# Decay logarithms from running sums by one product over 128 rows, and a running state that is kept turned

## The chip, the cores and the metric

The kernel is one program on one core of a Trainium2 chip. The metric is device time in microseconds (us) of one execution. Three runs of the kernel before gave 4488.98, 4490.3 and 4494.2 us, median 4490.3 us.

## The reference

The program computes one layer of a hybrid model in four steps, each `x = x + f(layernorm(x))`: a state-space mixer, a feed-forward part, a long convolution with a gate, and the same feed-forward part again. `x` is 8 sequences of 2048 tokens of 256 numbers. The change touches the mixer. For every sequence and every one of 8 heads it keeps a state `h` of 64 x 128 numbers:

```
B_proj, C_proj = turned by cos/sin of cumsum(dt * theta)   # 8 heads x 128
alpha = exp(dt_t * A_neg)
beta  = (1.0 - lam_t) * dt_t * alpha
gamma = lam_t * dt_t
h   = alpha * h + beta * Bx_prev + gamma * Bx_t            # Bx_t = u_t (64) times B_t (128)
y_t = einsum('bhpn,bhn->bhp', h, C_t)
```

`y` then goes through an RMS norm and an output projection. The kernel takes 128 tokens (a tile) at a time. Within a tile, token t gets from token s the product C_t.B_s times `exp(sum of the log alphas of s+1..t)`, and from all earlier tiles `exp(sum of log alphas up to t)` times C_t times the state at the tile's start. The sums of log alphas between two tokens are what the code calls decay logarithms; the state at the tile's start is the running state.

## The kernel before, in words

The program runs in five parts, one after the other: `normalise_tokens` (to about 124 us), `scan_and_filter` (to about 238 us), `mixer_and_first_ffn` (to about 3290 us), `long_convolution`, and `project_and_second_ffn`. In each part every engine has its own list of instructions, written out in order; the engines wait for one another on counting semaphores.

`scan_and_filter` makes all per-token numbers of the mixer for all 128 tiles at once: sigmoids, angles, sums of log alphas over tokens (TensorE products with the triangular matrices `upto` and `after`), exponentials of these. They are laid out in `params_all` (80 columns for each tile, `P_COS` to `P_ET`) and stored to DRAM. Two of the groups of eight columns (`P_A`) are the log alphas themselves, cut into two parts that add up to them.

`mixer_and_first_ffn` goes through the tiles in rounds of four (a quad). The list of one round is `body(tile, quad, n)`: for q = 0 to 3 it calls steps for tile 4n+q (lag 0), the tile before it (lag 1) and two before it (lag 2), and in between steps for whole quads (the first feed-forward part for quad n-1, the wide projection with its short filter for quad n-2). The calls stand in a fixed order for each engine. A step waits with `wait_for(engine, step, i)` until another step is done for tile i. Eight banks of PSUM are shared out: `bank_read` makes a writer wait until the former contents are read. The banks named here are `p_bc` (two), `p_tr` (transposes), `p_arg` (decay logarithms and the new state's product), `p_gram`, `p_y`, `p_post` (two, for the quad steps).

For a tile i the steps that the change touches, or that stand next to them, are these; g = 0, 1 is a group of four heads.
- POOL `masked_steps` (line 1050) multiplies `upto` by the log alphas of each head, twice (two parts): 128 x 512 numbers a time. PE `decay_logs` (lines 729 and 730) multiplies `after_r` by both and adds them up in `p_arg`. ACT `exponentials` (line 908) takes exp, ACT `own_bounds` (line 915) and DVE `cut_decay` (line 1173) bound the result, DVE `weigh_gram` multiplies it with the products C.B (`gram`, line 754).
- PE `turn_over` (line 744) transposes B and C by head through `p_tr`, ACT `copy_turned` (line 924) copies the bank to SBUF. There are four of these for a tile, over one bank.
- PE `outputs` (lines 769 and 772) makes y for four heads: the part from the tile and the part from `state`. It writes two heads beside each other, one into partitions 0 to 63 and one into 64 to 127.
- PE `new_state` (line 780) makes B times u for all eight heads, with B as the stationary operand of 128 x 128 and u as the moving one of 64 columns. POOL `fade_state` (line 1071) has multiplied the old state by its decay, DVE `carry_state` (line 1194) adds the product. `state` has n on the partitions and 8 x 64 columns.
- PE `project_u` (line 736) multiplies x with the weights of u. It stands right behind the last `turn_over` of the tile; behind it come `decay_logs` of group 1, and at q = 0 `x2n_over` (line 833), the transposes of the second layer norm's output, which ACT `normalised` (line 940) makes.

SP issues the loads; the DMAs of one round are the parts of x, `el` (exponentials by row), `par` (a quad's columns of `params_dram`) and the stores.

Of the kernel before, what the change touches and what calls it, by code (L numbers as in the profile page):

```python
# [6 lines left out]
F32 = mybir.dt.float32  # L7
F32R = mybir.dt.float32r
# [16 lines left out]
P_COS, P_SIN, P_A, P_G, P_RHO, P_W, P_EL, P_ET, P_ALL = 0, 8, 24, 40, 48, 56, 64, 72, 80  # L25
P_EARLY = P_G
# [207 lines left out]
def scan_and_filter(nc, ctx, t):  # L234
# [9 lines left out]
    a_hi = sb("sp_a_hi", [128, COLS], F32R)  # L244
# [26 lines left out]
    with nc.Block() as block:  # L271
        @block.sync
        def _(sp):
# [23 lines left out]
            sp.wait_ge(s["stored"], 64)  # L297

        @block.gpsimd
        def _(pool):  # L300
# [5 lines left out]
            g_.tensor_copy(t["after_r"][:, :], t["after"][:, :])  # L306
# [18 lines left out]
            g_.memset(taps[:, :, 0:TOK - 1], 0.0)  # L325
            pool.drain().then_inc(s["weights_done"], 1)

        @block.vector
        def _(dve):
# [44 lines left out]
            v_.tensor_copy(a_hi[:, :], arr["a"][:, :])  # L374
# [37 lines left out]
            v_.tensor_copy(col(P_A), as3(a_hi[:, :].bitcast(F32)))  # L412
            v_.tensor_tensor(col(P_A + HEADS), as3(arr["a"][:, :]), as3(a_hi[:, :].bitcast(F32)), ALU.subtract)
# [11 lines left out]
            dve.wait_ge(s["scan_act"], EXPS)  # L425
            by_seq = params[:, :, :].rearrange("p (b c) n -> p b c n", b=BATCH)
# [12 lines left out]
        def _(act):  # L439
# [32 lines left out]
        def _(pe):  # L472
# [38 lines left out]
            for b in range(BATCH):  # L511
                last = mm(pp[0][:, b * TOK:(b + 1) * TOK], arr["a"][:, b * 128:(b + 1) * 128], t["upto"][:, :], start=True, stop=True)
# [12 lines left out]
def mixer_and_first_ffn(nc, ctx, t):  # L525
# [4 lines left out]
    H64 = GROUP * HEAD_U  # L530
    QUAD = 4
    QUADS = TILES // QUAD
    SPAN = QUAD * TOK
    ident, upto, after, bound = t["ident"], t["upto"], t["after"], t["bound"]

    w_u, w_bc, in_w, after_r = t["w_u_sb"], t["w_bc_sb"], t["in_w_sb"], t["after_r"]
# [11 lines left out]
    steps = two("steps", [128, W4], F32R)  # L548
    decay, own, mix = two("decay", [128, W4]), two("own", [128, W4]), two("mix", [128, W4])
    u_g, u_w, state = sb("u_g", [128, 512]), sb("u_w", [128, 512]), two("state", [128, 512])  # L550
# [16 lines left out]
    names = ("project_b project_c rotate_b rotate_c turn_b turn_c over_b over_c copy_b copy_c steps logs exp diagonal own gram mix outputs take_y "  # L567
             "values gate_values weigh_values new_state fade carry_state split_hi split_rest sum_over mean_sq square_y pair_sums scan_rstd project_out "
             "residual1 rstd1 norm1 xn_over first_column shifted mixed key relu key_sq receptance tanh value gated residual2 rstd2 norm2 "
             "x2n_over x2_hi x2_lo widen took taps halo short_filter setup load_xnT0 load_xnT1 load_par0 load_par1 load_x0 load_x1 load_el0 load_el1 "  # L570
             "store_x2 store_x0 store_vx").split()
    BY_GROUP = set(names[:19])
# [19 lines left out]
    BANK_TR = (("over_c1", "copy_c1", 1, -1), ("over_b1", "copy_b1", 1, -1), ("over_c0", "copy_c0", 1, 0), ("over_b0", "copy_b0", 1, 0))  # L592
# [49 lines left out]
    with nc.Block() as block:  # L642
        @block.sync
        def _(sp):
# [30 lines left out]

            def load_x(n, pp):
# [16 lines left out]
            for i in range(2):  # L693
                load_xnT(i, Place(0, i, 0))
            load_par(0, 0)

            def body(tile, quad, n):
                for q in range(QUAD):
                    tile(q, -2, load_xnT)
                    tile(q, 0, load_el)  # L700
                    if q == 1:
                        quad(-1, load_par)
                        quad(2, store_x2)
                        quad(0, load_x)
# [1153 lines left out]
```

## Time and profile before

| what | value |
|---|---|
| median of three runs | 4490.3 us |
| profiled execution | 4485.84 us |
| its span (first to last instruction) | 4484.1 us |
| mean granted TensorE clock, of full speed | 0.978 |
| PE busy | 4197.9 us, 94% of the span |
| DVE busy | 3222.6 us, 72% |
| POOL busy | 2376.0 us, 53% |
| ACT busy | 2157.4 us, 48% |

Busy time is the time in which an engine runs at least one instruction. PE's matmuls overlap and their ends are modelled, so the cost of one in a dense sequence is read from the distance between two starts. PEld is TensorE's loading of the stationary operand, which overlaps the matmuls. The idle time of an engine says only something about the program's time where this engine's next instruction is on the path that sets the end.

### The profile page before, as it was taken

Reading aid. Unit: us, or ns where it says so; the run is one execution under the profiler, and the core shown is the slowest. Engines: PE = TensorE matmul, PEld = TensorE weight load, DVE = VectorE, ACT = ScalarE, POOL = GpSimd, SP = SyncE. Lnnn points to the kernel's source line nnn. Section 1 sums busy time; section 2 is a strip of 40 time slices with the busy share of each in tenths; the row PEclk is TensorE's granted clock in tenths of the full one; section 3 lists DMA queues with packets and bytes.
Section 4 is the critical chain, followed back from the end, with each engine's and each line's share of the span. In section 5 each row is a group of like instructions: output and inputs, shape, how many; then the busy total and the mean of one; then the engine's idle time right before and its main releaser. Section 6 shows DMA issues by size and latency. Waiting matters only on the chain. (4 is left out here: it accounts for less than half of the span.)

```text
span 4484.1 us, 118726 instructions
## 1 busy us (share of the span) xinstructions
PE 4197.9 (94%) x39924; PEld 3488.0 (78%) x39924; DVE 3222.6 (72%) x6737; ACT 2157.4 (48%) x5046; POOL 2376.0 (53%) x3284
## 2 busy tenths in 40 slices
PE   5389999999999999999999999999869999989999
PEld 3178788888888888878788788888648888878888
DVE  8867777777677776777767777677636666668888
ACT  3234444454444444444444444444446666645555
POOL 3276666666676666766666666666400000026666
PEclk9699999999999999999999999999979999989999
DMA  8321111111111111111111111111056666633333
GB/s 276 117 81 30 48 39 39 47 39 48 36 38 50 39 48 36 39 50 39 39 45 39 50 39 36 48 39 46 23 134 180 188 180 183 186 94 105 105 105 96
DMA packets 369774, 347.50 MB, mean 77 GB/s; under 512 B 24953, under 2 KB 343289, under 8 KB 360185
## 3 DMA queue, kind: packets, MB, share of 16 engines
q1 hardware_dynamic: 352380, 323.98, 24.2%
q10 hardware_dynamic: 16896, 16.78, 1.1%
q8 instruction: 324, 5.31, 0.5%
q14 instruction: 174, 1.43, 0.1%
HBM read 232.01 MB, written 108.66 MB: 76 GB/s over the span
## 5 line engine op out<-in xcount | busy, mean ns | idle before, releaser
L721 PE MATMUL bank<-w_bc,xnT 128*128 128x512 f32 x3072 | 804.3, 404 | 11.7 <-POOL xnT L1042 11.7
L924 ACT COPY turned_t<-bank 128x512 f32<-128x512 f32 x512 | 300.3, 587 | 982.4 <-PE bank L744 982.3
L721 PEld LDWEIGHTS bank<-w_bc,xnT 128*128 128x128 f32 x3072 | 556.8, 189 | 144.7 <-issue 34.5
L1455 PE MATMUL p_yc<-sig,toep 64*64 64x256 f32 (+14 forms) x16384 | 538.1, 282 | 13.7 <-issue 10.5
L1455 PEld LDWEIGHTS p_yc<-sig,toep 64*64 64x64 f32 x16384 | 475.1, 132 | 89.7 <-issue 43.5
L1050 POOL TENSOR_TENSOR steps<-upto,par 128x512 fp32r<-128x512 f32 x512 | 536.6, 1068 | 0.0
L1159 DVE TENSOR_TENSOR rot<-bank,par 128x512 f32<-128x512 f32 x512 | 350.1, 684 | 209.6 <-PE bank L721 124.7
L1059 POOL TENSOR_TENSOR turned_b<-rot 128x512 f32<-128x512 f32 x256 | 325.9, 1273 | 197.7 <-DVE rot L1160 197.5
L1604 POOL MEMSET xT<- 128x258 f32 x1 | 0.3, 314 | 684.2 <-POOLq L1349 684.2
L1059 POOL TENSOR_TENSOR turned_c<-rot 128x512 f32<-128x512 f32 x256 | 354.5, 1385 | 1.8 <-DVE rot L1160 1.8
L1160 DVE TENSOR_TENSOR rot<-bank,par 128x512 f32<-128x512 f32 x512 | 346.9, 677 | 0.0
L1248 DVE SCALAR_TENSOR_TENSOR conv<-bank,short,conv 128x511 f32<-128x511 f32 (+1 forms) x384 | 286.4, 746 | 69.7 <-ACT conv L980 55.4
L840 PE MATMUL bank<-x2T,in_w 128*128 128x512 f32 x1152 | 315.4, 410 | 18.7 <-issue 9.0
L915 ACT ACTIVATE own<-bound,par 128x128 f32<-128x128 f32 x1024 | 326.5, 400 | 0.4 <-DMA par<-params_dram 0.4
L1042 POOL TENSOR_TENSOR xnT<-xnT_raw,xnT 128x256 fp32r<-128x256 f32 x128 | 108.8, 850 | 384.2 <-ACT xnT L903 384.2
L1179 DVE TENSOR_TENSOR mix<-bank,decay 128x512 f32<-128x512 f32 x256 | 175.3, 685 | 180.1 <-PE bank L754 175.5
L754 PEld LDWEIGHTS bank<-turned_t 128*128 128x128 f32 x2048 | 265.3, 191 | 31.8 <-ACT turned_t L924 13.0
L754 PE MATMUL bank<-turned_t 128*128 128x128 f32 x2048 | 273.5, 276 | 0.7 <-DVE u_g L1167 0.4
L840 PEld LDWEIGHTS bank<-x2T,in_w 128*128 128x128 f32 x1152 | 214.9, 191 | 69.6 <-issue 21.4
L1487 DVE TENSOR_TENSOR ys<-p_yc,odd_y 64x256 f32<-64x256 f32 x256 | 95.6, 411 | 235.8 <-ACT odd_y L1406 235.8
L780 PEld LDWEIGHTS bank<-u_w,turned_b 128*128 128x128 f32 x2048 | 248.5, 192 | 10.3 <-issue 0.2
L1091 POOL TENSOR_TENSOR rstd<-var_eps,minus_half 128x2 f32<-128x2 f32 x128 | 90.7, 708 | 294.8 <-DVE var_eps L1205 291.7
(264 smaller groups left out, 9671.5 us busy)
## 6 DMA issues: line engine op xcount, KB each, us to landing
toep<-taps_dram SPq DMA_DIRECT2D x256, 260.0 KB, 4.1
el<-el_dram SPq DMA_DIRECT2D x256, 128.0 KB, 3.0
xg<-arg_x SPq DMA_DIRECT2D x32, 512.0 KB, 5.1
xnT_dram<-xt_g ACTq DMA_DIRECT2D x32, 512.0 KB, 5.4
xnT_raw<-xnT_dram SPq DMA_DIRECT2D x128, 128.0 KB, 2.5
x_quad<-arg_x SPq DMA_DIRECT2D x32, 512.0 KB, 3.9
x_dram<-x_quad SPq DMA_DIRECT2D x32, 512.0 KB, 3.7
x0T_dram<-conv SPq DMA_DIRECT2D x32, 512.0 KB, 2.8
```

What stands on the lines that cost most here:

```text
L721: last = mm(p_bc[c][:, :], xnT[w.q % 2][p][:, k, :], w_bc[q][:, k, c * 1024 + g * W4:c * 1024 + (g + 1) * W4], start=(n == 0), stop=(n == ...
L754: last = mm(p_gram[:, c], turned_t[g][0][:, c], turned_t[g][1][:, c], start=True, stop=True)
L780: last = mm(p_state[:, v], turned(w, h // GROUP, 0)[:, (h % GROUP) * STATE:(h % GROUP + 1) * STATE], u_w[:, v], start=True, stop=True)
L840: last = mm(p_post[W_BANK[e]][:, :], in_w[q][:, k, e * 128:(e + 1) * 128], x2T[p][:, k, :], start=(m == 0), stop=(m == len(SPLIT) - 1))
L915: last = s_.activation(own[g][:, h * TOK:(h + 1) * TOK], bound[:, :], ACT.Identity, scale=par[w.p][:, w.q, P_RHO + g * GROUP + h:P_RHO + g ...
L924: s_.copy(turned_t[g][c][:, :], p_tr[:, :]).then_inc(s[f"copy_{BC[c]}"], 1)
L1050: last = g_.tensor_tensor(heads(steps[p][:, :]), upto[:, :].unsqueeze(1).broadcast_to([128, GROUP, TOK]), over(of_group(P_A + p * HEADS, w ...
L1059: g_.tensor_tensor(turned(w, g, c)[:, :], rot1[c][:, :], rot2[c][:, :], ALU.add).then_inc(s[f"turn_{BC[c]}"], 1)
L1159: v_.tensor_tensor(heads(rot1[c][:, :]), heads(p_bc[c][:, :]), cos, ALU.mult)
L1160: v_.tensor_tensor(parts(rot2[c][:, :]), parts(p_bc[c][:, :])[:, :, ::-1, :], over(sin.rearrange("p (h s) -> p h s", s=2), STATE // 2), AL ...
L1248: last = v_.scalar_tensor_tensor(out=conv[:, e, back:], in0=p_post[W_BANK[e]][:, 0:SPAN - back], scalar=short[:, e, 2 - back:3 - back], in ...
L1455: last = mm(by_seq(p_y[p][c][odd * H:(odd + 1) * H, 0:2 * TILES])[:, :, first:], toep[n % SLOTS][c * H:(c + 1) * H, lag * H:(lag + 1) * H] ...
```

## The change: what it does, and the diff

The decay logarithm between s and t is now the difference of two running sums, cum[t] - cum[s]. `scan_and_filter` makes the running sums for all tiles (row = tile and head, column = token), splits them into four pieces so that each is held well in the reduced format `F32R`, and stores them in `cum_dram`. In the mixer one product over 128 rows gives the logarithms of four heads: of its rows, 48 are 4 pieces times (8 rows for heads: cum[s] on one side, minus one for the head on the other; 4 rows for the tiles of the quad: cum[t] on one side, a one for the tile on the other), 16 are zero, and 64 put -1e30 where t < s for pairs of tokens. The fixed rows come from a new input `pick` by two loads at the part's start and are copied by ACT into `sums_s` and both buffers of `sums_t`; SP loads the other rows for each quad by eight DMAs (`load_sums`). `masked_steps`, `P_A` and `after_r` are gone.

The running state is now accumulated as `state_p`, with u on the partitions (two heads above each other) and n in the columns. `new_state` has u as the stationary operand of 64 columns and B as the moving one of 128. `outputs` still needs the other layout, so PE turns the state for each tile (`turn_state`, four transposes through `p_tr`) and ACT copies it (`copy_state`).

```diff
-P_COS, P_SIN, P_A, P_G, P_RHO, P_W, P_EL, P_ET, P_ALL = 0, 8, 24, 40, 48, 56, 64, 72, 80
+P_COS, P_SIN, P_G, P_RHO, P_W, P_EL, P_ET, P_ALL = 0, 8, 24, 32, 40, 48, 56, 60
+PIECES, GRID = 4, 98304.0
 # scan_and_filter, SP
+            for p in range(PIECES):
+                sp.dma_start(t["cum_dram"][p].rearrange("(b c) n -> c b n", c=128), cum[p][:, :].rearrange("c (b n) -> c b n", b=BATCH)).then_inc(s["stored"], 16)
 # scan_and_filter, POOL, at its end
+            pool.wait_ge(s["scan_dve"], LOGS)
+            g_.tensor_scalar(coarse[:, :], arr["a"][:, :], GRID, None, ALU.add)
+            g_.tensor_scalar(coarse[:, :], coarse[:, :], GRID, None, ALU.subtract)
+            g_.tensor_tensor(fine[:, :], arr["a"][:, :], coarse[:, :], ALU.subtract)
 # scan_and_filter, DVE
-            v_.tensor_copy(a_hi[:, :], arr["a"][:, :])
-            v_.tensor_copy(col(P_A), as3(a_hi[:, :].bitcast(F32)))
-            v_.tensor_tensor(col(P_A + HEADS), as3(arr["a"][:, :]), as3(a_hi[:, :].bitcast(F32)), ALU.subtract)
             dve.wait_ge(s["scan_act"], EXPS)
+            for k in range(2):
+                v_.tensor_tensor(cum[2 * k + 1][:, :].bitcast(F32R), pp[1 + k][:, :], cum[2 * k][:, :], ALU.subtract)
 # scan_and_filter, ACT
-            s_.activation(col(P_EL), as3(pp[0][:, :]), ACT.Exp).then_inc(s["scan_act"], 1)
+            s_.activation(col(P_EL), as3(pp[0][:, :]), ACT.Exp)
             s_.activation(col(P_W), as3(pp[1][:, :]), ACT.Exp)
-            s_.activation(col(P_ET), as3(pp[2][:, :]), ACT.Exp)
+            for e in range(2):
+                rows = slice(e * HEAD_U, (e + 1) * HEAD_U)
+                s_.activation(params[rows, :, P_ET:P_ET + HEADS // 2], as3(pp[2][rows, :])[:, :, e::2], ACT.Exp)
+            act.drain().then_inc(s["scan_act"], 1)
             act.wait_ge(s["scan_pe"], ROWS)
             s_.activation(el_rows, pp[0][:, :].rearrange("p (b n) -> p b n", b=BATCH), ACT.Exp)
+            for k in range(2):
+                s_.copy(cum[2 * k][:, :].bitcast(F32R), pp[1 + k][:, :])
 # scan_and_filter, PE
-            for b in range(BATCH):
-                last = mm(pp[0][:, b * TOK:(b + 1) * TOK], arr["a"][:, b * 128:(b + 1) * 128], t["upto"][:, :], start=True, stop=True)
+            for dst, src in ((pp[0], arr["a"]), (pp[1], coarse), (pp[2], fine)):
+                for b in range(BATCH):
+                    last = mm(dst[:, b * TOK:(b + 1) * TOK], src[:, b * 128:(b + 1) * 128], t["upto"][:, :], start=True, stop=True)
 # mixer, SP; load_sums(0, 0) behind load_par(0, 0), then quad(-1, load_sums) behind quad(-1, load_par) at q == 1
+            def load_sums(n, pp):
+                wait(sp, s["picked"], 1)
+                wait_for(sp, "logs1", QUAD * (n - 1) - 1)
+                for p in range(PIECES):
+                    tiles = t["cum_dram"][p, n * SPAN // TOK * HEADS:(n + 1) * SPAN // TOK * HEADS, :]
+                    at = p * (HEADS + QUAD)
+                    sp.dma_start(sums_t[pp][at + HEADS:at + HEADS + QUAD, :, :].bitcast(F32), ...)
+                    sp.dma_start(sums_s[at:at + HEADS, pp * QUAD:(pp + 1) * QUAD, :].bitcast(F32), ...)
+            sp.dma_start(gate[:, :, :], t["pick"][0:128]...).then_inc(s["load_pick"], 16)
+            sp.dma_start(k_sq[:, :, :], t["pick"][128:256]...).then_inc(s["load_pick"], 16)
             load_par(0, 0)
+            load_sums(0, 0)
 # mixer, PE
             def decay_logs(i, w, g):
-                wait_for(pe, f"steps{g}", i)
+                wait(pe, s["picked"], 1)
+                wait(pe, s[f"load_sums{w.p}"], 16 * 2 * PIECES * (w.n // 2 + 1))
                 bank_read(pe, BANK_ARG, f"logs{g}", i)
-                mm(p_arg[:, :], after_r[:, :], steps[0][:, :], start=True, stop=False)
-                mm(p_arg[:, :], after_r[:, :], steps[1][:, :], start=False, stop=True).then_inc(s["logs"], 1)
+                mm(p_arg[:, :], sums_s[:, w.p * QUAD + w.q, :], sums_t[w.p][:, g, :], start=True, stop=True).then_inc(s["logs"], 1)
             def outputs(i, w, g):
-                wait_for(pe, "carry_state", i - 1)
+                wait_for(pe, "copy_state", i - 1)
             def new_state(i, w):
                 for h in range(HEADS):
-                    last = mm(p_state[:, v], turned(w, h // GROUP, 0)[:, ...], u_w[:, v], start=True, stop=True)
+                    pair, e = h // 2, h % 2
+                    last = mm(p_state[e * 64:(e + 1) * 64, pair * STATE:(pair + 1) * STATE], u_w[:, h * HEAD_U:(h + 1) * HEAD_U],
+                              turned(w, h // GROUP, 0)[:, ...], start=True, stop=True)
+            def turn_state(i, w):
+                wait_for(pe, "carry_state", i)
+                bank_read(pe, BANK_TR, "turn_state", i + 1)
+                for pair in range(4):
+                    c = slice(pair * 128, (pair + 1) * 128)
+                    last = tp(p_tr[:, c], state_p[1 - w.q % 2][:, c], ident[:, :])
+                last.then_inc(s["turn_state"], 1)
                     tile(q, 0, project_u)
+                    tile(q, 1, turn_state)
 # mixer, ACT
+            def copy_state(i, w):
+                wait_for(act, "turn_state", i)
+                wait_for(act, "outputs1", i - 1)
+                s_.copy(state[1 - w.q % 2][:, :], p_tr[:, :]).then_inc(s["copy_state"], 1)
+            act.wait_ge(s["load_pick"], 32)
+            s_.copy(sums_s[:, :, :], flat_k.rearrange("r (m n) -> r m n", n=TOK))
+            for p in range(2):
+                s_.copy(sums_t[p][:, :, :], flat_gate.rearrange("r (g n) -> r g n", g=GROUPS))
+            act.drain().then_inc(s["picked"], 1)
                     tile(q, 0, copy_turned, 0, 0)
+                    tile(q, 1, copy_state)
 # mixer, POOL (masked_steps and its two calls are gone)
             def fade_state(i, w):
-                wait_for(pool, "outputs1", i - 1)
-                g_.tensor_tensor(all_heads(state[1 - w.q % 2][:, :]), all_heads(state[w.q % 2][:, :]), over(param(P_ET, w), HEAD_U),
+                wait_for(pool, "turn_state", i - 2)
+                g_.tensor_tensor(heads(state_p[1 - w.q % 2][:, :]), heads(state_p[w.q % 2][:, :]), over(par[...][P_ET ...], STATE),
 # mixer, DVE
-                v_.tensor_tensor(state[1 - w.q % 2][:, :], p_state[:, :], state[1 - w.q % 2][:, :], ALU.add)
+                v_.tensor_tensor(state_p[1 - w.q % 2][:, :], p_state[:, :], state_p[1 - w.q % 2][:, :], ALU.add)
```

At q = 0 the new `copy_state` stands on ACT between `copy_turned` and `normalised(2, 1)`, at q = 1 ahead of `normalised(1, 0)`, `normalised(1, 1)` and `take_up 4`.

## Rows read from the trace of the kernel before

**Rows 1.** The page's 40 slices of the span: busy tenths.
```profile
PE   5389999999999999999999999999869999989999
```
**Rows 2.** Busy time by window: start:end, length, then each engine, clock, DMA share, GB/s.
```profile
1000.00:1500.00 500.00, 488.77 (x3125) 403.43 (x3124) 362.08 (x646) 233.80 (x544) 331.79 (x402) 1.00 0.14 43
```
**Rows 3.** Groups by line: busy us, mean ns of one, idle before.
```profile
L1050 POOL TENSOR_TENSOR steps<-upto,par 128x512 fp32r<-128x512 f32 x512 | 536.6, 1068 | 0.0
L1173 DVE TENSOR_TENSOR decay<-decay,own 128x512 f32<-128x512 f32 x256 | 241.9, 945 | 0.0
```
**Rows 4.** Timeline of PE at q = 1 of a round: start, us, engine, line.
```profile
1073.37 1.64 PE L840 MATMUL bank<-x2T,in_w 128*128 128x512 f32 x6
1074.93 0.44 PE L772 MATMUL bank<-mix,u_g 128*64 128x128 f32 x4
...
1075.96 1.66 PE L721 MATMUL bank<-w_bc,xnT 128*128 128x512 f32 x6
1077.45 1.56 PE L840 MATMUL bank<-x2T,in_w 128*128 128x512 f32 x6
1078.85 1.89 PE L780 MATMUL bank<-u_w,turned_b 128*128 128x64 f32 x16
1080.58 0.61 PE L744 MATMUL bank<-ident,turned_c 128*128 128x128 f32 x4
...
1088.57 0.39 PE L729 MATMUL bank<-steps,after_r 128*128 128x512 f32 x1
...
1089.04 1.56 PE L840 MATMUL bank<-x2T,in_w 128*128 128x512 f32 x6
```
**Rows 5.** Timeline of all engines at q = 0 of the same round.
```profile
1053.02 1.37 DVE L1237 SCALAR_TENSOR_TENSOR x_quad<-gate,x_quad 128x512 f32<-128x512 f32 x1 [0.17 <-issue]
1059.60 0.66 PE L744 MATMUL bank<-ident,turned_b 128*128 128x128 f32 x4
1060.01 1.64 PE L736 MATMUL bank<-w_u,xnT 128*128 128x512 f32 x6
1060.29 0.59 ACT L924 COPY turned_t<-bank 128x512 f32<-128x512 f32 x1
1060.37 0.68 DVE L1194 TENSOR_TENSOR state<-bank,state 128x512 f32<-128x512 f32 x1
1061.49 0.39 PE L729 MATMUL bank<-steps,after_r 128*128 128x512 f32 x1
1061.78 1.09 ACT L940 ACTIVATE xn<-x_quad,shift,rstd 128x256 f32<-128x256 f32 x2 [0.91 <-POOL shift L1094]
1062.93 1.41 PE L833 MATMUL bank<-ident,xn 128*128 128x128 f32 x8 [0.81 <-ACT xn L940]
```
**Rows 6.** Timeline of the mixer's start, all engines.
```profile
238.14 0.81 SPq L657 DMA_DIRECT2D xnT_raw<-xnT_dram  x2
240.20 0.87 ACT L903 CAST xnT<-xnT_raw 128x256 fp32r<-128x256 f32 x2 [16.09 <-DMA xnT_raw<-xnT_dram]
241.80 1.30 SPq L665 DMA_DIRECT2D el<-el_dram  x2
247.47 0.40 PE L729 MATMUL bank<-steps,after_r 128*128 128x512 f32 x1
```
**Rows 7.** Timeline of the scan part, all engines.
```profile
152.19 1.04 ACT L453 CAST w_u<-params_all 128x1024 fp32r<-128x1024 f32 x1
...
168.61 2.30 DVE L374 CAST sp_a_hi<-sp_a 128x1024 fp32r<-128x1024 f32 x1
...
198.01 2.05 PE L512 MATMUL p_sp<-upto,sp_a 128*128 128x128 f32 x16 [1.11 <-ACT params_all L458]
...
203.46 1.04 ACT L466 ACTIVATE sp_dt<-sp_m 128x1024 f32<-128x1024 f32 x1
...
212.75 0.69 DVE L422 COPY params_all<-sp_dt 128x1024 f32<-128x1024 f32 x1
...
215.90 0.33 SPq L292 DMA_DIRECT2D params_dram<-params_all  x1
```

More of the change, by code:

```diff
@@ L565, in mixer_and_first_ffn @@
     p_state = p_arg
[L567 to L568 removed]
+    names = ("project_b project_c rotate_b rotate_c turn_b turn_c over_b over_c copy_b copy_c logs exp diagonal own gram mix outputs take_y "
+             "values gate_values weigh_values new_state fade carry_state turn_state copy_state split_hi split_rest sum_over mean_sq square_y pair_sums scan_rstd project_out "
              "residual1 rstd1 norm1 xn_over first_column shifted mixed key relu key_sq receptance tanh value gated residual2 rstd2 norm2 "
[L570 removed]
+             "x2n_over x2_hi x2_lo widen took taps halo short_filter setup load_xnT0 load_xnT1 load_par0 load_par1 load_x0 load_x1 load_el0 load_el1 load_sums0 load_sums1 load_pick picked "
              "store_x2 store_x0 store_vx").split()
[L572 removed]
+    BY_GROUP = set(names[:18])
     s = {n: ctx.enter_context(nc.semaphore(n)) for n in names}
@@ L1043, in split_xnT @@
                                  ALU.subtract).then_inc(s["split_rest"], 1)
-            def masked_steps(i, w, g):
-                wait_loaded(pool, "load_par", w)
-                wait_for(pool, f"logs{1 - g}", i - 1 + g)
-                for p in range(2):
-                    last = g_.tensor_tensor(heads(steps[p][:, :]), upto[:, :].unsqueeze(1).broadcast_to([128, GROUP, TOK]),
-                                            over(of_group(P_A + p * HEADS, w, g), TOK), ALU.mult)
-                last.then_inc(s["steps"], 1)
             def add_turned(i, w, g, c):
@@ L1125, in body @@
                     tile(q, 2, pair_sums)
-                    tile(q, 0, masked_steps, 0)
                     tile(q, 0, add_turned, 0, 1)
@@ L1131, in body @@
                     tile(q, 2, scan_rstd)
-                    tile(q, 0, masked_steps, 1)
                     tile(q, 0, add_turned, 1, 1)
@@ L1193, in carry_state @@
                 wait_for(dve, "new_state", i)
-                v_.tensor_tensor(state[1 - w.q % 2][:, :], p_state[:, :], state[1 - w.q % 2][:, :], ALU.add).then_inc(s["carry_state"], 1)
+                v_.tensor_tensor(state_p[1 - w.q % 2][:, :], p_state[:, :], state_p[1 - w.q % 2][:, :], ALU.add).then_inc(s["carry_state"], 1)
             def moments(which, places, src, by):
@@ L1802, in build @@
                 t["scal"] = early.enter_context(nc.sbuf_tensor("scal", [128, TILES, 24], F32))
+                for n in ("upto", "after", "nxt", "wrap"):
+                    t[n] = early.enter_context(nc.sbuf_tensor(n, [128, 128], F32))
                 with ExitStack() as c:
@@ L1835 @@
     decay = _np.exp(-where[None, :] * _np.abs(deltas)[:, None]).astype(f32)
+    eye, half = _np.eye(HEADS), _np.arange(TOK // 2)[:, None]
+    none, four = _np.zeros((4, HEADS)), _np.tile(_np.eye(4), 2)
+    heads, tiles = (_np.concatenate([_np.tile(_np.concatenate(part), (PIECES, 1)), _np.zeros((16, HEADS))]).repeat(TOK, axis=1)
+                    for part in ((-eye, none), (0 * eye, four)))
+    token = _np.arange(HEADS * TOK)[None] % TOK
+    pick = _np.concatenate([heads, _np.where(token < 2 * half, -1e30, 0.0), tiles, _np.where(token // 2 == half, 1.0, 0.0)]).astype(f32)
     arrays = {
```

47 lines of the change are left out of this document (29 added, 18 removed).

## The prediction
> **What bounds the kernel now.** I read the page first: in the slices of the mixer (the fourth to the twenty-ninth) PE stands at 9 tenths or more nearly throughout [rows 1]. The busy time by window says the same with numbers: in 500 us of the mixer PE is busy for 488.77, DVE for 362, POOL for 332, ACT for 234, at a clock of 1.00 [rows 2]. So an edit in the mixer is worth what it changes in PE's queue, plus what it makes PE wait for. The groups by line name the largest thing removed: POOL's `masked_steps`, 536.6 us, more than any other group of POOL, with no idle time before it [rows 3]. It lies beside PE, so by itself it is worth nothing. The timelines then give PE's cost per step as distances between starts [rows 4], the one place per quad where PE waits for ACT [rows 5], the mixer's start [rows 6] and the scan [rows 7]. The profiled execution took 4485.84 us, 4.5 us under the median of 4490.3; I work out a difference and take it off the median.
>
> **PE per tile.** *Logarithms.* The two products of a group take 0.47 us from the first's start to the next instruction's (1088.57 to 1089.04) [rows 4]; one remains, with the same 128 x 512 shape. It saves 0.235 for a group, 0.47 a tile.
>
> *New state.* Sixteen instructions (two for each of eight heads) take 1.73 us (1078.85 to 1080.58) [rows 4]. The trace has the new form already: `outputs` is sixteen instructions with a stationary operand of 128 x 64 and a moving one of 128 columns, two heads side by side in alternation, and takes 1.03 us (1074.93 to 1075.96) [rows 4]. Getting into that form costs something too: six `widen` products ahead of it take 1.56 us from start to start (1073.37 to 1074.93), the same six ahead of `new_state` 1.40 (1077.45 to 1078.85) [rows 4]. So 1.03 + 0.16 = 1.19, which saves 0.54. The ends: 0 if the heads of a pair don't overlap, 0.7 if entry is free; I take 0.55.
>
> The Trainium skill speaks to this twice ("TensorEngine Tiling (Array Packing)"). Under "When to Use Tiling" it advises to swap stationary and streaming operand and tile the columns where the free size is 64 or less; by its factor of two the saving would be half of 1.73, 0.87 us. Under "Key Properties" it says that a change of tiling mode drains TensorE, which speaks against the change. The rows agree with the second (the 0.16 at the entry) and give less than the first.
>
> *Turning the state.* Four transposes of 128 x 128 take 0.41 us (1059.60 to 1060.01) [rows 5], so +0.41; from 0.35 to 0.45 by its neighbours.
>
> Sum per tile: -0.47 - 0.55 + 0.41 = -0.61 us; for 128 tiles -78 us. Ends: -0.70 to -0.50, that is -90 to -64, as long as the heads of a pair overlap.
>
> **What `turn_state` waits for.** It waits for ACT to have read the bank (the copy of the tile's last `turn_over`) and for `carry_state`. At q = 0 `project_u` starts at 1060.01 and covers PE until 1061.49; the copy runs from 1060.29 to 1060.88 and `carry_state` ends at 1061.05 [rows 5]. The copy has 0.6 us to spare. It keeps the same distance from `project_u` whatever PE saves earlier, so I take no wait. If that cover went, it would cost up to 0.9 us a tile (the copy's end less `project_u`'s start). `carry_state` is DVE's: at q = 0 it comes late because DVE has been running without a pause. There POOL's absence helps, since the residual's multiply-add took 1.37 us at 1053.02 [rows 5] beside POOL's products, where DVE's addition to the state, also 128 x 512, took 0.68, and L1173, which also reads and writes SBUF alone, takes 945 ns in the mean [rows 3]. I credit DVE with 0.7 to 1.0 us at q = 0, so `carry_state` ends near 1060.2, before `project_u`. If it does not, q = 0 loses 0.4 us more.
>
> **What is queued behind `copy_state`.** ACT is in order. At q = 0 `normalised(2, 1)` stands behind it, and PE's `x2n_over` waits for that: today it starts at 1062.93, 0.05 us after the norm has ended (1061.78 + 1.09) [rows 5], while PE was ready 0.8 us before. In the new order: `project_u` ends 0.55 earlier at least for the new state, about 1060.9 (of the 0.235 of group 0 I count nothing here: the Gram products behind it wait for a copy); `turn_state` takes PE to 1061.3; ACT's copy starts some 0.25 later and takes 0.6, to 1062.15; the norm takes 1.09, to 1063.2. So `x2n_over` starts at about 1063.25, 0.3 later than today, although PE has 0.6 less to do. At q = 0 the tile gives back 0.6 + 0.3 = 0.9 us, in the 30 quads that have both steps: +27 us. Ends: 0 (if the POOL chain to the norm gets so early that the order on ACT is all that counts, and ACT is quicker than I think) and +40 (with a late `carry_state`). At q = 1 the copy and two norms stand ahead of `take_up 4`, so DVE's taps come about 2 us later. Counting forward from `project_u`'s end, DVE's first rotation ends just before PE's third projection needs its bank; I take 0, at most 0.3 a quad (+10). At q = 2 and 3 what follows on ACT also waits for later PE work: nothing.
>
> **The mixer's start.** The first logarithms start at 247.47 [rows 6]. Now SP issues the x parts (238.14 to 238.95), the two loads of `pick` (0.5 each), `par`; `pick` is 1 MB and should be in at about 243.5; ACT copies 128 x 1024 numbers three times at 1.04 each [rows 7], to 246.7. Only then does SP issue eight loads, at 0.65 each (two take 1.30) [rows 6], to 251.9, and the last lands about 2 us later, at 254: PE waits 6.5 us. After it PE's clock may be down for a while; with 1.5 for that, +8 us (ends +4 and +14).
>
> **The scan.** Removed from DVE: the rounding of `a` (2.30 us) and two passes into `params_all`, about 1.8 [rows 7]. The chain by ACT and PE grows: two more sets of eight products at 2.05, two copies at 1.04, two exponentials (about 1 each) that PE now waits for: +8.2. It ended at 204.5 (the second sine) and DVE needs it at 212.75 [rows 7]; now it comes at 204.5 - 2.4 + 8.2 = 210.3, against DVE at 208.6, so DVE waits 1.7, and then has two subtractions more (0.7 to 2.3 each by the rows, say 1.2). `params_dram` starts at 215.90 [rows 7] -4.1 + 1.7 + 2.4, the same time. The stores grow by 2 MB and shrink by 1.3, with four more issues on SP before the taps: +1.5 us (-1 to +6).
>
> **Elsewhere.** Each quad SP issues eight loads more (5 us) ahead of `store_x2`, `load_x` and the next x part. The data come a quad ahead, so I count nothing; it would show as a PE wait for DMA. POOL loses 536.6 / 128 = 4.2 us a tile [rows 3], worth only the relief of DVE above. The convolution and the last part are untouched.
>
> Sum: -78 + 27 + 8 + 1.5 = -41.5; 4490.3 - 41.5 = 4449 us. Own range: 4425 to 4475.
>
> **Rivals.**
> *A: nothing is given back at q = 0.* PE's savings count in full because the relieved DVE and POOL also bring the norm early, and the start costs 4. For it: DVE is the engine that runs without pause there, and it gets faster. Against: the copy and the norm stand one behind the other on ACT, and no relief shortens these two. -85 + 5 + 5 = -75: 4415 us.
> *B: a pair's heads don't overlap in `new_state` (slower).* Its products then take 16 x 0.11 = 1.73 us or more plus the entry of 0.16: per tile -0.47 + 0.16 + 0.41 = +0.10, for 128 tiles +13, and +36 with the terms for q = 0, start and scan: 4526 us. It decides from a block of 1.52 us on (41.5 / 128 = 0.33 above 1.19). Against it: the same shapes and the same alternation in `outputs`.
> *C: `turn_state` isn't covered.* If ACT reaches the last copy late in most tiles, PE waits up to 0.9: half of that is +58, 4507 us. The 0.6 to spare in the rows speaks against it.
> *D: the removal does nothing and the additions cancel.* PE stays at its pace because waits that I don't see fill the savings: 4485 to 4495.
> The skill names a rule that gives DVE's relief another weight ("SBUF — State Buffer", "Who interferes with whom"): DVE and GpSimd take turns at a shared port pair, the loser blocked for the whole instruction. The row of 1.37 us, twice the 0.68 of its neighbour, agrees; by it the relief is at the upper end of my 0.7 to 1.0, which moves the forecast less than a microsecond a quad.
>
> **How the numbers follow.** Forecast 0.67, A 0.17, B 0.04, C 0.05, D 0.07. A measurement of this kernel can tell about 0.2%, 9 us, from no change. Faster than 4481: forecast nearly whole and A, 0.84 to 0.87; within: D, and the forecast's tail, 0.06; slower: B, C, 0.08. The range for 8 in 10 takes in the forecast's bounds and A's: 4415 to 4478.
>
> **What would show it.** The new state's products in about 1.2 us a tile with their entry; one logarithm product a group; four transposes right behind `project_u` with no idle time before them; at q = 0 an idle time of about 1.9 us before `x2n_over`, ended by ACT's norm; PE's first logarithms at about 254 instead of 247.5; DVE's L1173 nearer 700 ns. Wrong would be: idle time before `turn_state`, `new_state` above 1.5 us, a quad longer than today's, or a scan that ends more than 6 us later.

## The result, and the profile after

The changed kernel takes 4546.2 us (median of 4 runs, 4542.9 to 4551.9) against 4490.2 for the kernel before: 1.0125 times as long, with a 95% interval of 1.0109 to 1.0141. It is 56 us slower; I had forecast 41 us faster, and the time lies 68 us above the top of my range. The profiled execution took 4551.91 us, 5.7 above the median, with a span of 4550.2 and a mean granted clock of 0.966 (before: 4485.84, 4484.1 and 0.978).

The page's slices first, answering to [rows 1]:
```profile
PE   5389999999999999999999999999859999989999
...
POOL 3345445444454444444444444445300000026666
```
PE's row is the same but for the thirtieth slice, 5 where it was 6. A slice is 114 us, more than a quad, so tenths can't show what happens once in each quad. The same 500 us as [rows 2], in the kernel after:
```profile
1000.00:1500.00 500.00, 480.71 (x3124) 383.36 (x3123) 359.01 (x640) 240.18 (x559) 234.51 (x312) 0.98 0.13 41
```
POOL lost 97 us of its work, PE is busy for 8.1 us less, and the clock is no longer 1.00. PE stands still for longer, and part of its work runs at a lower clock.

The groups by line answer to [rows 3], with the new state's products in their new form (busy us, mean ns of one, idle before):
```profile
L812 PE MATMUL bank<-turned_b,u_w 128*64 128x128 f32 x2048 | 140.0, 279 | 0.0
L1216 DVE TENSOR_TENSOR decay<-decay,own 128x512 f32<-128x512 f32 x256 | 214.9, 839 | 0.8 <-ACT decay L949 0.8
L1280 DVE SCALAR_TENSOR_TENSOR x_quad<-gate,x_quad 128x512 f32<-128x512 f32 x64 | 103.0, 1609 | 12.9 <-issue 12.7
```
One group of DVE got faster (945 to 839 ns), and one slower: the residual's multiply-add, 1609 ns in the mean. In the kernel before the same group reads
```profile
L1237 DVE SCALAR_TENSOR_TENSOR x_quad<-gate,x_quad 128x512 f32<-128x512 f32 x64 | 64.9, 1014 | 10.4 <-issue 10.2
```
PE's waits between 450 and 3100 us (us in total, times, longest), first after, then before:
```profile
PE bank L873 <- ACT xn L986: 40.0, 28, 1.4
PE bank L821 <- DVE state_p L1237: 32.0, 28, 1.2
```
```profile
PE bank L833 <- ACT xn L940: 23.3, 28, 0.9
```
Both waits come once in each of 28 quads. The second is new: `turn_state` waits for `carry_state`, 1.15 us a quad. The first, for the norm, grew from 0.83 to 1.43.

Where they come from is seen in the timeline of q = 0 (start, us, engine, line), answering to [rows 5]:
```profile
1063.04 2.96 PE L753 MATMUL bank<-w_bc,xnT 128*128 128x512 f32 x12
...
1071.74 1.28 POOL L1104 TENSOR_TENSOR turned_c<-rot 128x512 f32<-128x512 f32 x1
1071.88 1.69 DVE L1280 SCALAR_TENSOR_TENSOR x_quad<-gate,x_quad 128x512 f32<-128x512 f32 x1 [0.17 <-issue]
...
1077.20 1.27 POOL L1104 TENSOR_TENSOR turned_b<-rot 128x512 f32<-128x512 f32 x1 [0.94 <-DVE rot L1203]
1077.29 1.73 DVE L1280 SCALAR_TENSOR_TENSOR x_quad<-gate,x_quad 128x512 f32<-128x512 f32 x1 [0.16 <-issue]
...
1078.31 1.64 PE L768 MATMUL bank<-w_u,xnT 128*128 128x512 f32 x6
...
1080.35 0.69 DVE L1237 TENSOR_TENSOR state_p<-bank,state_p 128x512 f32<-128x512 f32 x1
...
1081.10 0.66 PE L821 MATMUL bank<-ident,state_p 128*128 128x128 f32 x4 [1.15 <-DVE state_p L1237]
...
1081.79 0.58 ACT L970 COPY state<-bank 128x512 f32<-128x512 f32 x1 [2.61 <-PE bank L821]
...
1082.27 1.09 ACT L986 ACTIVATE xn<-x_quad,shift,rstd 128x256 f32<-128x256 f32 x2
...
1083.41 1.83 PE L873 MATMUL bank<-ident,xn 128*128 128x128 f32 x8 [1.43 <-ACT xn L986]
...
1084.89 4.08 PE L753 MATMUL bank<-w_bc,xnT 128*128 128x512 f32 x12
```
And three rows of the kernel before at the same place:
```profile
1054.77 2.03 POOL L1050 TENSOR_TENSOR steps<-upto,par 128x512 fp32r<-128x512 f32 x2
...
1058.10 0.69 DVE L1237 SCALAR_TENSOR_TENSOR x_quad<-gate,x_quad 128x512 f32<-128x512 f32 x1 [0.16 <-issue]
...
1059.16 1.27 POOL L1059 TENSOR_TENSOR turned_b<-rot 128x512 f32<-128x512 f32 x1
```
Before, `masked_steps` held POOL back, so that `turned_b` of group 1 began 0.37 us after the residual had finished in 0.69. Now POOL is idle, takes `turned_b` up at once, 0.09 us ahead of DVE's second residual, and this takes 1.73 us: it ends 0.55 us after POOL's instruction. `carry_state` is late by that, PE waits, `copy_state` is late, and the norm stands behind it. The last row is the third loss: twelve projection products take 4.08 us. Twelve such products take 2.96 at 1063.04. The windows there (engines, clock):
```profile
1078.00:1083.00 5.00, 2.83 (x15) 1.91 (x15) 4.48 (x13) 1.80 (x4) 2.44 (x9) 1.00 0.00 0
1083.00:1087.00 4.00, 3.59 (x13) 2.92 (x14) 1.50 (x3) 3.46 (x9) 1.48 (x3) 0.59 0.37 104
1087.00:1091.00 4.00, 4.00 (x24) 3.46 (x24) 3.33 (x6) 1.15 (x3) 2.62 (x4) 0.98 0.46 158
```
PE is busy for 2.83 of 5 us, and in the 4 us behind that the granted clock is 0.59: mostly the lower level, 1.2 GHz. The trace after has such a stretch behind each of the 28 `x2n_over` between 450 and 3100 us (not behind the one before them, at 416), the trace before behind none. This count, "low in n of 28", is used below for every run.

Cut at the first and the last `x2n_over`, the two profiled executions differ by 66.1 us: 10.3 before the first, 46.7 between them, 9.1 behind the last. "A quad" below is the mean distance of these starts: 93.94 us before, 95.51 after, +1.57. From the start of q = 0 to `x2n_over` it is 18.78 before and 20.37 after, +1.59; all the rest of the quad cancels.

### The profile page after: what moved, and what is told of

Read it like the earlier page. It is cut to its first block and busy times, and to the rows that moved or that the text cites. A ratio compares the mean times of both kernels' runs of the same rounds, so it can differ in the third digit from the quotient of the medians.

```text
span 4550.2 us, 119987 instructions
## 1 busy us (share of the span) xinstructions
PE 4199.4 (92%) x40212; PEld 3406.1 (75%) x40212; DVE 3223.3 (71%) x6736; ACT 2217.5 (49%) x5180; POOL 1855.1 (41%) x2776
## 5 line engine op out<-in xcount | busy, mean ns | idle before, releaser
L753 PE MATMUL bank<-w_bc,xnT 128*128 128x512 f32 x3072 | 837.0, 416 | 15.3 <-POOL xnT L1096 15.1
L753 PEld LDWEIGHTS bank<-w_bc,xnT 128*128 128x128 f32 x3072 | 583.3, 198 | 160.3 <-issue 45.6
L1104 POOL TENSOR_TENSOR turned_c<-rot 128x512 f32<-128x512 f32 x256 | 344.0, 1344 | 38.9 <-DVE rot L1203 38.9
L1096 POOL TENSOR_TENSOR xnT<-xnT_raw,xnT 128x256 fp32r<-128x256 f32 x128 | 94.9, 742 | 485.9 <-ACT xnT L944 485.9
L833 PE MATMUL bank<-w_out,yT 128*128 128x256 f32 x1024 | 244.6, 382 | 0.7 <-issue 0.3
L1216 DVE TENSOR_TENSOR decay<-decay,own 128x512 f32<-128x512 f32 x256 | 214.9, 839 | 0.8 <-ACT decay L949 0.8
```

Of the source, the lines that this page charges most:

```text
L753: last = mm(p_bc[c][:, :], xnT[w.q % 2][p][:, k, :], w_bc[q][:, k, c * 1024 + g * W4:c * 1024 + (g + 1) * W4], start=(n == 0), stop=(n == ...
L833: last = mm(p_post[OUT_BANK[q]][:, 0:DIM], yT[w.q % 2][:, k * TOK:(k + 1) * TOK], w_out[:, k, :], start=(k == 0), stop=(k == 3))
L1104: g_.tensor_tensor(turned(w, g, c)[:, :], rot1[c][:, :], rot2[c][:, :], ALU.add).then_inc(s[f"turn_{BC[c]}"], 1)
L1216: v_.tensor_tensor(decay[g][:, :], decay[g][:, :], own[g][:, :], ALU.min).then_inc(s["own"], 1)
```

## The experiments

My theory when I began: the whole loss per quad is two orders at q = 0. POOL's `turned_b` meets DVE's second residual (price: `carry_state`'s 1.09 us), ACT's copy stands ahead of the norm, and the two waits together cost the clock. Rivals: one part of the change is bad by itself, or POOL's relief is not the cause and DVE is late for another reason. Each was timed in three rounds. Line numbers shift by a few between the kernels.

**1. POOL's order alone.** In the kernel after:
```diff
                         quad(2, layer_rstd, 2, 0)
+                        quad(2, layer_rstd, 2, 1)
                     tile(q, 0, add_turned, 1, 0)
                     if q == 0:
-                        quad(2, layer_rstd, 2, 1)
```


> The changed kernel, but at q = 0 POOL makes turned_b of group 1 behind layer_rstd(2, 1) instead of ahead of it, so that DVE's second residual runs with POOL idle. Theory of the collision: that residual takes 0.7 us instead of 1.66, carry_state ends 1 us earlier in each quad, PE's wait for it falls from 1.3 to 0.3 us: 30 quads give 30 us, and up to 70 if the clock then stays up: 4475 to 4516 us. Rival (the added steps themselves cost this): no change, 4546 us within 9.

Measured: 4487.3 us, 0.9989 of before (0.9980 to 0.9999). The timeline at q = 0:
```profile
1062.49 0.69 DVE L1280 SCALAR_TENSOR_TENSOR x_quad<-gate,x_quad 128x512 f32<-128x512 f32 x1 [0.16 <-issue]
1064.51 0.69 DVE L1237 TENSOR_TENSOR state_p<-bank,state_p 128x512 f32<-128x512 f32 x1
...
1065.81 1.27 POOL L1104 TENSOR_TENSOR turned_b<-rot 128x512 f32<-128x512 f32 x1
...
1067.58 1.37 PE L873 MATMUL bank<-ident,xn 128*128 128x128 f32 x8 [1.43 <-ACT xn L986]
```
POOL's `turned_b` starts 1.3 us after `carry_state`, the residual takes 0.69 again, and 59 us come back by one line. A quad takes 93.47, low-clock stretches stand in 6 of 28. The quads of this one kernel that begin with such a stretch take 94.7 in the mean, the others 93.2. The work is the same: it was where it stood.

**2. ACT's order alone, and 3. both.**
```diff
-                    tile(q, 1, copy_state)
                     if q == 0:
                         quad(2, normalised, 2, 1)
+                    tile(q, 1, copy_state)
```


> The changed kernel, but at q = 0 ACT does normalised(2, 1) ahead of copy_state. Theory of the collision: DVE is as late as before; the norm starts when POOL's shift is there, 0.5 us earlier: 15 us, or 55 if the clock then stays up: 4490 to 4530 us. Rival (the copy in ACT's order is the cause): PE's 1.4 us wait before x2n_over goes almost whole: 30 x 1.4 = 42 us or more, 4500 us, with the wait for carry_state left as it is.

> Both orders of the two runs before. Theory of the collision: both waits nearly gone, clock stays at full: a quad takes 93.9 - 1.7 to 93.9 - 0.8 us, with the start's 10.5 us the program ends at 4450 to 4480 us. Rival (added steps): not under 4500 us.

Measured: 4516.2 us (1.0061, 1.0044 to 1.0078) and 4464.3 (0.9944, 0.9928 to 0.9961). ACT's order is worth 30 us, both together 82, a little less than the sum. In 2 PE still waits 1.15 at `turn_state`, and 0.91 before `x2n_over`, and the clock is low in 14 of 28. With both, the clock of the window is 1.00 again and there is no low stretch:
```profile
1000.00:1500.00 500.00, 487.03 (x3209) 388.27 (x3208) 362.32 (x654) 246.05 (x576) 247.82 (x319) 1.00 0.14 44
```

**4. The waits kept and filled.** To part the clock's share from the waits', PE gets work that nobody reads, in the two places where it waits at q = 0, with the late engines left as they are: 12 transposes of the unit matrix before `turn_state`'s wait for `carry_state`, and group 1's logarithm product repeated 5 times.
```diff
-                    tile(q, 1, turn_state)
+                    tile(q, 1, turn_state, 12 if q == 0 else 0)
...
-                    tile(q, 0, decay_logs, 1)
+                    tile(q, 0, decay_logs, 1, 5 if q == 0 else 0)
```


> The changed kernel, but at q = 0 PE repeats twelve transposes of a constant (about 1 us) while it waits for carry_state, and five products of the logarithms (about 1.15 us) while it waits for the norm; nothing else changes. If the clock's fall in each quad is a cost of its own: granted clock 1.00 in the mixer, a quad about 1.3 us shorter, 30 x 1.3 = 40 us: 4506 us. If only the waits count: 4546 us, or a little more.

Measured: 4518.0 us (1.0056, 1.0039 to 1.0072), 28 us less than after although PE has more to do, and 12 more than the 4506 that I expected. `x2n_over` starts 20.38 us after the start of q = 0, where it was 20.37: the late engines are as late as before. A quad takes 94.33, so -1.18, and the window's clock is 1.00:
```profile
1000.00:1500.00 500.00, 490.72 (x3252) 393.21 (x3251) 364.97 (x649) 243.77 (x567) 240.52 (x316) 1.00 0.13 41
```
So PE's standing still is what brings the clock down, and the clock alone is worth 1.2 us a quad by this run, and about 1.5 by the two kinds of quad in run 1 and in run 6 below (94.9 and 93.3 there).

**5. POOL kept busy.** In place of `masked_steps`, POOL multiplies 128 x 256 numbers three times per group into a tile that nobody reads.
```diff
+            def spare_steps(i, w, g):
...
+                for p in range(3):
+                    pool.drain()
+                    g_.tensor_tensor(spare..., bound..., par..., ALU.mult)
...
+                    tile(q, 0, spare_steps, 1)
                     tile(q, 0, add_turned, 1, 1)
```


> The changed kernel with idle work given back to POOL: where masked_steps stood, three multiplications of 128 x 256 numbers into a tile that nobody reads (some 2.3 us a group, 4.6 us a tile). Theory of the collision: turned_b of group 1 comes late again at q = 0, DVE's second residual takes 0.7 us again, carry_state is 1 us earlier, so more work on POOL makes the kernel faster: 4480 to 4515 us. Rival (POOL's removal helps or does nothing, the added steps cost): 4546 us or more.

Measured: 4549.1 us (1.0137, 1.0120 to 1.0154). The expectation is missed: giving POOL its load back helps nothing. The timeline says why:
```profile
1078.68 0.77 DVE L1292 SCALAR_TENSOR_TENSOR x_quad<-gate,x_quad 128x512 f32<-128x512 f32 x1 [0.16 <-issue]
...
1080.48 1.27 POOL L1114 TENSOR_TENSOR turned_b<-rot 128x512 f32<-128x512 f32 x1
...
1080.67 1.10 DVE L1260 TENSOR_SCALAR var_eps<-mean_var 128x2 f32<-128x2 f32 x1
...
1081.69 0.68 DVE L1249 TENSOR_TENSOR state_p<-bank,state_p 128x512 f32<-128x512 f32 x1
```
This residual is nearly free (0.77; 0.74 in the mean), as meant, but `turned_b` now meets a DVE instruction of 128 x 2 numbers, which takes 1.10 us where it takes 0.17 in the kernel after (1.10 or 1.11 in 20 of 28 quads, 0.43 in 7). It ends with POOL's (1081.77 and 1081.75), and `carry_state` is as late as ever. The first residual is still hit too, by `fade_state` (1.60 in the mean). The second residual's collision moved behind it, to the last instruction of its statistics. "POOL less busy is the cause" would be too short: the place in time counts, not the load.

**6. The logarithms alone, and 7. the turned state alone.** Each is the kernel after with the other part put back as before (the `masked_steps` and two products a group in 7; new state in the old form, no `turn_state` and `copy_state` in 6).
```diff
 (6)
-                    tile(q, 1, turn_state)
...
-                    tile(q, 1, copy_state)
...
+                    last = mm(p_state[:, v], turned(w, h // GROUP, 0)[...], u_w[:, v], ...)
```
```diff
 (7)
+                    tile(q, 0, masked_steps, 1)
                     tile(q, 0, add_turned, 1, 1)
```


> Only the logarithms by one product (with its loads and stores), the state as in the kernel before. PE saves 0.47 us a tile and nothing is added to it. Theory of the collision: POOL is as empty as in the changed kernel, so DVE's second residual is hit, x2n_over starts about 1.1 us later after the start of q = 0, the other three tiles save 1.4: a quad 0.3 us shorter, plus 10.5 at the start: 4485 to 4495 us, up to 4530 if PE's waits lower the clock. Rival (the turned state is what costs): -60 + 10 = 4440 us.

> Only the turned state, the logarithms as in the kernel before, POOL as full as before. PE saves 0.55 - 0.41 = 0.14 us a tile. Theory of the collision: no collision (second residual 0.7 us), but the norm stands behind the copy: x2n_over 0.3 to 0.6 us later, the other tiles save 0.4: 4485 to 4500 us. Rival (the turned state is what costs): near the changed kernel, 4535 us.

Measured: 4514.6 us (1.0056, 1.0039 to 1.0073) and 4515.9 (1.0063, 1.0046 to 1.0080). Each costs 25 us by itself, by its own half of the mechanism. In 6 there is no `turn_state`, but the residuals take 1.38 and 1.65 in the mean, PE waits 0.47 for `carry_state` ahead of group 1's logarithms and 1.12 before `x2n_over`, and the clock is low in 17 of 28 (a quad 94.20, and the whole of the later start). In 7 the second residual takes 0.69 and the clock never falls; the first takes 1.60 beside `fade_state` (1.38 before), and copy and norm stand in series: PE waits 0.38 at `turn_state` and 1.20 before `x2n_over`, where it was 0 and 0.83 before; a quad takes 94.73, and the start is as before. I had expected at most 10 us of 7, with 0.14 us saved a tile. Nothing is saved: from the first Gram product behind `x2n_over` to the start of the next q = 0 it is 71.12 us, where it was 71.11 before and is 69.74 in 6. The saving outside q = 0 is all the logarithms'.

**8. Both residuals free.** ACT as in 2, and POOL at q = 0 in an order that puts each large instruction where DVE has none that meets it (for q = 1 to 3 the order stays, in the `else` branch):
```diff
-                    tile(q, 1, fade_state)
-                    tile(q, 2, scan_rstd)
-                    tile(q, 0, add_turned, 1, 1)
                     if q == 0:
+                        tile(q, 0, add_turned, 1, 1)
+                        tile(q, 2, scan_rstd)
                         quad(2, layer_rstd, 2, 0)
+                        tile(q, 1, fade_state)
+                        quad(2, layer_rstd, 2, 1)
+                    else:
...
                     tile(q, 0, add_turned, 1, 0)
                     if q == 0:
-                        quad(2, layer_rstd, 2, 1)
```


> The changed kernel with ACT's norm ahead of the copy, and at q = 0 a POOL order that keeps its 128 x 512 products away from both residuals of DVE: turned_c of group 1 ahead, fade_state behind layer_rstd(2, 0), turned_b last. Theory of the collision: the first residual takes 0.7 us too (1.68 in all runs so far), DVE's chain to the norm is 0.8 to 1 us shorter: a quad 91.8 us instead of 92.65: about 4440 us. Rival (what is left is the order on ACT and PE's own work): 4464 us.

Measured: 4432.8 us, 0.9878 of before (0.9861 to 0.9894), the fastest of all: 57 us under the kernel before. A quad takes 91.66. The timeline:
```profile
1044.96 1.27 POOL L1104 TENSOR_TENSOR turned_c<-rot 128x512 f32<-128x512 f32 x1
...
1046.62 0.69 DVE L1284 SCALAR_TENSOR_TENSOR x_quad<-gate,x_quad 128x512 f32<-128x512 f32 x1 [0.17 <-issue]
...
1051.01 0.69 DVE L1284 SCALAR_TENSOR_TENSOR x_quad<-gate,x_quad 128x512 f32<-128x512 f32 x1 [0.16 <-issue]
...
1053.03 0.69 DVE L1241 TENSOR_TENSOR state_p<-bank,state_p 128x512 f32<-128x512 f32 x1
...
1054.33 1.28 POOL L1104 TENSOR_TENSOR turned_b<-rot 128x512 f32<-128x512 f32 x1
...
1054.52 0.60 PE L821 MATMUL bank<-ident,state_p 128*128 128x128 f32 x4
...
1055.56 1.37 PE L873 MATMUL bank<-ident,xn 128*128 128x128 f32 x8 [0.21 <-ACT xn L986]
```
`carry_state` ends at 1053.72, 0.8 before the turning; no idle time stands before `turn_state`, and 0.21 before `x2n_over`, where it was 1.43 after and 0.81 before.

**9. The same order in the kernel before**, with `masked_steps` left in. It asks how much of 8 is the order and how much the change.
```diff
-                    tile(q, 1, fade_state)
-                    tile(q, 2, scan_rstd)
-                    tile(q, 0, masked_steps, 1)
-                    tile(q, 0, add_turned, 1, 1)
                     if q == 0:
+                        tile(q, 2, scan_rstd)
+                        tile(q, 0, masked_steps, 1)
+                        tile(q, 0, add_turned, 1, 1)
                         quad(2, layer_rstd, 2, 0)
+                        tile(q, 1, fade_state)
+                        quad(2, layer_rstd, 2, 1)
+                    else:
...
                     tile(q, 0, add_turned, 1, 0)
                     if q == 0:
-                        quad(2, layer_rstd, 2, 1)
```


> The kernel before, with the POOL order of e8 as far as it goes: at q = 0 fade_state behind layer_rstd(2, 0) and turned_b of group 1 last; masked_steps stays. If e8's lead over the kernel before is mostly the order on POOL: a quad 92.5 us or less, 4445 us. If it is mostly the work taken from PE (2.3 us a quad) and POOL's two products still hit the first residual: a quad 93.3 to 93.9, 4470 to 4490 us.

Measured: 4473.7 us, 0.9959 (0.9944 to 0.9974). The order alone is worth 17 us to the old kernel; the change on top of it 41. Both residuals take 0.69 here too, where I had thought that POOL's two products would hit the first. A quad takes 93.37 here and 91.66 in 8: 30 times 1.71 is 51, less the start's 10.

**10. `carry_state` ahead of the second residual on DVE**, in the kernel after.
```diff
-                    if q == 0:
-                        quad(2, residual2, 1)
...
                     tile(q, 1, carry_state)
+                    if q == 0:
+                        quad(2, residual2, 1)
```


> The changed kernel, but at q = 0 DVE does carry_state ahead of the second residual. PE's wait of 1.3 us before turn_state should go, and the norm comes 0.6 us later by DVE while the copy comes earlier. If the norm's chain (residual, POOL's rstd, ACT) is what ends last: x2n_over starts at the same time within 0.3 us, a quad 95.2 to 95.8, 4546 us within 9. If the wait for carry_state is the cost: 30 x 1.3 = 39 us less, 4507 us.

Measured: 4525.3 us (1.0089, 1.0060 to 1.0117), between what the two accounts gave. PE no longer waits at `turn_state`, but 2.27 us in the mean before `x2n_over`, for the norm, whose input the residual is: it still collides in part (1.14 us) and comes later. The clock is low in 22 of 28. `carry_state` now runs beside POOL's `turned_b`, and isn't slowed:
```profile
1071.49 0.68 DVE L1237 TENSOR_TENSOR state_p<-bank,state_p 128x512 f32<-128x512 f32 x1
...
1071.65 1.27 POOL L1104 TENSOR_TENSOR turned_b<-rot 128x512 f32<-128x512 f32 x1 [0.93 <-DVE rot L1203]
```
Both chains matter, and moving one instruction on DVE only trades them.

## Why the prediction was wrong

*The step that failed:* "I credit DVE with 0.7 to 1.0 us at q = 0, so `carry_state` ends near 1060.2, before `project_u`." Counted from the start of q = 0, `carry_state` starts at 16.21 us in the kernel before and at 17.30 after: 1.09 later, not 0.7 to 1.0 earlier. I had seen in [rows 5] that a residual beside POOL's work takes 1.37 and a free one 0.69, and concluded that less work on POOL means fewer meetings. The reading was wrong already in the kernel before. What the first residual met at 1053.02 was not `masked_steps`, which came at 1054.77 when it was through, but `fade_state`, which the change keeps:
```profile
1052.80 1.04 POOL L1071 TENSOR_TENSOR state<-state,par 128x512 f32<-128x512 f32 x1
```
And the second residual, the one just ahead of `carry_state`, took 0.69 before: there was nothing to gain on it. Then, POOL's order is fixed and its instructions start when their input is there: without `masked_steps` the additions `turned_c` and `turned_b` moved forward onto the two residuals, of which the first had met the shorter `fade_state` and the second nothing large (means 1.38 and 0.69; after 1.68 and 1.65). Runs 1, 3 and 8 show it, run 5 that POOL's load isn't the variable.

The Trainium skill had the rule for it ("SBUF — State Buffer", "Who interferes with whom"): an instruction of DVE with two inputs in SBUF contends with one of GpSimd (POOL here) that reads SBUF, the order of issue decides who is blocked, and one with a single input there does not contend, unless it is in a mode that uses both of DVE's port pairs. The rows agree in all three: 1.73 against 0.69 for the residual, POOL's issued 0.09 ahead; `carry_state`, with one input in PSUM, keeps its 0.68 beside `turned_b` in run 10. The blocked 128 x 2 instruction of run 5 has a single input in SBUF; it is a `tensor_scalar`, which the Trainium skill lists there among those that can enter such a mode, and no run here shows in which mode it ran. I used the rule to weigh a relief; it should have sent me to the start times.

*What followed in ACT's queue.* Forecast: norm behind the copy, +0.3 a quad, 0.9 given back in all. The mechanism was right, the size was not: the wait for `carry_state` came on top, so PE waits 1.15 + 1.43 at q = 0 where I had 0 + 1.9. "If it does not, q = 0 loses 0.4 us more" was my price for a late `carry_state`; the runs put it near 2 us (run 1: 95.51 to 93.47 a quad, 0.96 of it up to `x2n_over` and 1.1 in the products behind, by the clock).

*The clock.* I had a term for it only at the start. PE's two waits, whose ends lie 2.3 us apart, lower the clock once in each quad, 1.33 us from start to start (0.29 for `x2n_over`, 1.04 for the twelve products), 1.18 by run 4 with the filling, about 1.5 by the two kinds of quad in runs 1 and 6. In a kernel at 1.00 throughout [rows 2] I should have priced an idle time twice: by its length, and by what it does to the clock.

*PE per tile.* Forecast -0.61. The timeline of q = 1, answering to [rows 4]:
```profile
1003.45 1.56 PE L880 MATMUL bank<-x2T,in_w 128*128 128x512 f32 x6
1004.95 1.09 PE L812 MATMUL bank<-turned_b,u_w 128*64 128x128 f32 x16
1005.97 0.66 PE L776 MATMUL bank<-ident,turned_c 128*128 128x128 f32 x4
...
1012.61 0.60 PE L821 MATMUL bank<-ident,state_p 128*128 128x128 f32 x4
1012.96 1.65 PE L880 MATMUL bank<-x2T,in_w 128*128 128x512 f32 x6
1014.45 0.39 PE L762 MATMUL bank<-sums_t,sums_s 128*128 128x512 f32 x1
1014.68 1.57 PE L880 MATMUL bank<-x2T,in_w 128*128 128x512 f32 x6
```
New state: 1.02 from start to start instead of 1.73, and 1.50 instead of 1.40 for the six products ahead, so -0.61 with its entry: rival B is out, the heads of a pair overlap. One logarithm product: 0.23, as forecast. Turning: 0.35 here, 0.41 at q = 0, as forecast, and 0.54 at q = 2, above my 0.45. What I had no term for is the way back into the old form: the transposes behind the new state take 0.05 more (0.16 at q = 2), and the products behind the turning 0.09 more. Group 0 at q = 0 saved 0.04 only. Over the three tiles without the waits 1.35 us were saved, 0.45 a tile: 0.16 short. Runs 6 and 7 say where: the logarithms alone save 1.37 there, near my 0.47 a tile, and the turned state, for which I had 0.14 a tile, nothing. The Trainium skill ("TensorEngine Tiling (Array Packing)", "When to Use Tiling") gives a factor of two at this width; the rows show 1.7, and 1.5 with the entry.

*The start.* +8 and +1.5 forecast, 10.3 measured. The sum was right, the parts less so:
```profile
243.94 0.81 SPq L674 DMA_DIRECT2D xnT_raw<-xnT_dram  x2
...
250.40 1.05 ACT L1031 CAST sums_s<-k_sq 128x1024 fp32r<-128x1024 f32 x1 [3.96 <-DMA k_sq<-arg_pick]
...
253.39 0.27 SPq L699 DMA_DIRECT2D sums_t<-cum_dram  x1
...
257.94 0.77 PE L762 MATMUL bank<-sums_t,sums_s 128*128 128x512 f32 x1 [4.19 <-DMA sums_s<-cum_dram]
```
The mixer begins 5.8 us later (I had 1.5), by the scan's stores: `cum_dram` holds SP for 14.16 us, so the stores of the taps behind it are issued 2.5 us later (233.28 for 230.74), and from the end of their issue to the first load it is 7.6 us where it was 4.4. The eight loads issue in some 0.3 us each, not 0.65; PE waits 4.19 for them, not 6.5.

*The sum, mended.* Against the forecast a quad lost 1.29 more than planned at q = 0 up to `x2n_over` (run 1, with the second residual free, gives back 0.96 of it), 1.33 by the clock, and 0.48 by the smaller saving on PE: 3.1, times 30 is 93, and 4449 + 93 = 4542, the measured 4546 but for 4. The parts overlap a little (run 4 has 1.18 for the clock). Another 9.1 us of the profiled execution lie behind the last `x2n_over`, in code that the change doesn't touch. That stretch took between 1214 and 1226 us over all the runs, without order; what sets it stays open.

*The rivals.* C had the right place and the wrong cause: `turn_state` isn't covered, but at q = 0 alone, and by DVE, not ACT. A is nearly what run 8 is, where nothing is given back at q = 0; it ends at 4433 and not at 4415 because PE saves less. D is out, since the savings are all seen in the timeline. None of my cases had a POOL instruction that comes earlier and blocks.

## What to carry to other kernels

When work is taken off an engine that shares a resource with a critical one, don't credit the relief: redo the start times, and see which of its remaining instructions now meets which. Price an idle time of PE in a loop also by the clock behind it, and look at the window's clock before and after. If the mechanism is a collision, its order is one line: here the same work went from +56 to -57 us by four moved calls, one on ACT and three on POOL.

## What the runs showed of the hardware that I had not expected

A DVE instruction of 128 x 2 numbers took 1.10 us instead of 0.17 behind an addition of POOL's (run 5): it ended with POOL's (1081.77 and 1081.75), so a tiny instruction can wait as long as a large one. The residual ends 0.55 us after POOL's in every meeting with an addition of POOL's that began first: both residuals in each of 28 quads after, the first in run 1. In run 9 POOL's product began 0.3 us behind the residual, and this took its 0.69.

PE's clock followed waits of one or two microseconds, once a quad. With 1.15 and 1.43 us, shortly one after the other, it was low in 28 of 28; with 2.27 alone in 22 (run 10), with 0.47 and 1.12 in 17 (run 6), with 1.15 and 0.91 in 14 (run 2), with 1.43 alone or nearly so in 6 (run 1), with 0.38 and 1.20 in none (run 7). Runs 6 and 7 have nearly the same waits, so their lengths alone don't set the count; what else does stays open. Filling the waits with products that nobody reads made the kernel 28 us faster (run 4).
